# A graph network's last layer: message rows as weights, two source blocks a step, sums turned afterwards

## The reference, cut to what matters

```python
xs = x[src]; xd = x[dst]
att = sigmoid(xs @ W_att[:d] + xd @ W_att[d:] + b_att)      # one number an edge
messages = (xs @ W_msg + b_msg) * att
aggregated = segment_sum(messages, dst, num_segments=num_nodes)
# then a GRU of aggregated and x, and a batch norm
```

## Time and profile before

| | us |
|---|---|
| median of 3 runs (lowest, highest) | 6111.06 (6102.99, 6115.57) |
| the profiled execution | 6071.99 |
| its span, first to last instruction | 6069.9 |

### The profile page before, as it was taken

One profiled execution on the slowest core, in us unless ns is written; L12 is line 12 of the kernel. 1 busy time (PEld: TensorE's weight loads), 2 busy tenths in 40 slices (PEclk: granted clock), 3 DMA queues, 4 the chain that ended last, 5 costly groups with the idle time before them and its releaser, 6 DMA issues.

```text
span 6069.9 us, 111610 instructions
## 1 busy us (share of the span) xinstructions
PE 5266.9 (87%) x30743; PEld 3838.3 (63%) x30744; DVE 3972.0 (65%) x10172; ACT 2815.2 (46%) x7038; POOL 1738.2 (29%) x1720
## 2 busy tenths in 40 slices
PE   3788888999999997888888887999988998888888
PEld 2444447888888884444444445666666667777775
DVE  4999994443433335666666776555555556999996
ACT  3577772111111116777767775222222225666664
POOL 1000000000000003666666655666666660000001
PEclk8899999999999997898988887999999999999999
DMA  3355555555555532111111112333333331222220
GB/s 92 123 162 160 161 160 201 186 184 179 189 183 205 191 142 66 46 46 46 46 45 46 47 38 76 88 88 87 88 88 88 88 87 70 87 109 88 100 90 22
DMA packets 396064, 650.40 MB, mean 107 GB/s; under 512 B 99831, under 2 KB 338386, under 8 KB 370639
## 3 DMA queue, kind: packets, MB, share of 16 engines
q1 hardware_dynamic: 330844, 526.22, 25.9%
q0 software_dynamic: 54832, 117.48, 7.5%
q10 hardware_dynamic: 10052, 2.53, 0.2%
HBM read 511.57 MB, written 134.42 MB: 106 GB/s over the span
## 4 chain that ended last, share of the span: by engine, by line
PE 66%; DVE 13%; issue 9%; ACT 4%; SPq 3%; DMA 2%; DVEq 1%; another core or an unknown queue 1%; POOL 1%; ACTq 0%; POOLq 0%
PE ps L1523 20%; PE ps L1579 12%; PE ps L1714 6%; PE ps L1633 5%; PE ps L1642 4%; DVE scaled L1109 4%; PE ps L1649 3%; DVE rg L836 3%; PE ps L1635 3%; SPq L478 3%; PE ps L1636 2%; PE ps L1578 2%; PE ps L1507 2%; PE ps L1421 2%; DMA A_d<-scaled 1%
## 5 line engine op out<-in xcount | busy, mean ns | idle before, releaser
L551 POOL DMA_INDIRECT rg<-tab_L,idxT x1664 | 1649.8, 991 | 3137.5 <-DMA tab_L<-planes 2257.6
L1523 PE MATMUL ps<-planes 128*128 128x384 bf16 (+1 forms) x7350 | 1225.7, 327 | 20.1 <-DVE planes L849 16.7
L1523 PEld LDWEIGHTS ps<-planes 128*128 128x128 f16 (+1 forms) x7350 | 1036.8, 142 | 173.1 <-issue 23.5
L1265 ACT ACTIVATE scaled<-onehot,rg 128x128 f32<-128x128 f32 x2912 | 892.8, 388 | 372.9 <-PE ps L1579 190.1
L1579 PE MATMUL ps<-scaled,rg 128*128 128x512 f32 x1664 | 1018.0, 704 | 0.0
L1714 PE MATMUL ps<-planes,scaled 128*128 128x128 f32 (+1 forms) x4900 | 757.5, 298 | 89.5 <-DVE scaled L1109 89.3
L1578 PEld LDWEIGHTS ps<-rg,onehot 128*128 128x128 f32 x1664 | 335.4, 212 | 731.9 <-issue 385.3
L1109 DVE TENSOR_TENSOR scaled<-scaled,planes 128x256 f32<-128x256 f32 x1225 | 777.0, 720 | 10.6 <-DMA planes<-A_d 7.4
L1714 PEld LDWEIGHTS ps<-planes,scaled 128*128 128x128 f32 (+1 forms) x4900 | 628.7, 190 | 209.8 <-DVE scaled L1109 104.5
L1347 ACT ACTIVATE scaled<-ps,att 128x256 f32<-128x256 f32 x1225 | 568.7, 474 | 257.2 <-DVE scaled L1109 213.8
L1208 ACT ACTIVATE scaled<-ps 128x392 f16 x1184 | 549.7, 500 | 266.9 <-DMA A_d<-scaled 117.6
(11 more groups left out here) (257 smaller groups left out, 6334.4 us busy)
## 6 DMA issues: line engine op xcount, KB each, us to landing
planes<-A_d SPq DMA_DIRECT2D x196, 1568.0 KB, 8.2
A_d<-scaled SPq DMA_DIRECT2D x1184, 98.0 KB, 1.7
planes<-rows_d SPq DMA_DIRECT2D x209, 256.0 KB
rg<-tab_L,idxT POOLq DMA_INDIRECT x1664
real_row<-real_d SPq DMA_DIRECT2D x200, 32.0 KB, 4.1
planes<-w_d SPq DMA_DIRECT2D x209, 9.0 KB
tab_L<-planes SPq DMA_DIRECT2D x7, 476.0 KB, 3.1
x_keep<-planes SPq DMA_DIRECT2D x7, 448.0 KB, 3.1
```

What stands on the lines that cost most here:

```text
L551: pool.indirect_dma_start(ring[:, q * GROUP + g, 0:width], None, table[:, :], bass.IndirectOffsetOnAxis(idxT[:, at:at + 1], 0)).then_inc(g ...
L1265: last = act.activation(scaled[:, s % 4, m * P:(m + 1) * P], onehot[:, q % 2, g, :], ACT.Copy, scale=ring[:, s, D + m:D + m + 1])
L1523: last = pe.matmul(ps_agg(u), a_blk[n % ABUF][:, 0:w, k], q_rows[l % 2][:, k].rearrange("p t n -> p (t n)"), start=(k == 0), stop=(k == BL ...
```

## The change

Source blocks are taken in 25 double steps (`TWOS`), the last with one block. In each, ACT makes two gates, written side by side: `gate` is now `(set i, destination n, block k)` with k innermost and 2 long, so that ACT writes with a step of 8 bytes. DVE multiplies both with one instruction of 512 elements; of `c_blk` it reads two neighbouring fp16 at each destination. `weight` has three buffers, in the tensors `dlT`, `dlLT` and `idxT`, which hold nothing any more by then.

PE's product is turned round. The message rows of a block are the stationary operand, and the weighted counts of 256 destinations are streamed, with a step of 8 bytes. The sums come out with features on partitions (`ps_pair`). So they are turned: ACT copies them to SBUF at step `AT_LEAVE` = 1 of the next pair (`pair_sum`, semaphore `turn_in`), PE transposes them at `AT_TURN` = 3 (`turned`), and DVE's splits at 4 and 6 wait for that. The other places are halved.

```diff
-AT_PREP, AT_ATT, AT_SPLIT, AT_FOLD, AT_AGG = 28, 36, (2, 6), (16, 20), (20, 24)
+TWOS = -(-BLOCKS // 2)
+IN_TWO = [min(2, BLOCKS - 2 * h) for h in range(TWOS)]
+AT_PREP, AT_ATT, AT_LEAVE, AT_TURN, AT_SPLIT, AT_FOLD, AT_AGG = 14, 18, 1, 3, (4, 6), (9, 11), (11, 13)
...
-        gate = scaled[:, 0:2, :].rearrange("p a n -> p (a n)").rearrange("p (b k n) -> p b k n", b=4, k=2)
-        weight = scaled[:, 2:4, :].rearrange("p a n -> p (a n)").rearrange("p (b k n) -> p b k n", b=4, k=2)
-        ps_rows = lambda u: ps[0:VB_COLS[u], u % 4, 0:P]
+        gate = scaled[:, :, :].rearrange("p b (i n k) -> p b i n k", i=2, k=2)
+        weight = [t.rearrange("p (i n k) -> p i n k", i=2, k=2) for t in (dlT[:, 0:4 * P], dlLT[:, 0:4 * P], idxT[:, 0:4 * P].bitcast(fp32))]
+        ps_pair = lambda q: ps[:, q % 2, 0:2 * P]
+        pair_sum = [t[:, 4 * P:6 * P] for t in (dlT, dlLT)]
+        ps_rows = lambda u: ps[0:VB_COLS[u], 2 + u % 2, u // 2 % 2 * P:(u // 2 % 2 + 1) * P]
...
@@ DVE, split @@
-                dve.wait_ge(pair_done, BLOCKS * (u // 2 + 1))
+                dve.wait_ge(turned, u // 2 + 1)
...
@@ DVE, the loop @@
-                        if t >= 4:
-                            dve.wait_ge(pair_done, t - 3)
-                        dve.tensor_tensor(weight[:, t % 4], gate[:, t % 4], c_blk[:, 2 * q % ABUF:2 * q % ABUF + 2, :, k], ALU.mult).then_inc(weighted, 1)
+                        if t >= 3:
+                            dve.wait_ge(pair_done, t - 2)
+                        n = IN_TWO[k]
+                        dve.tensor_tensor(weight[t % 3][:, :, :, 0:n], gate[:, t % 4, :, :, 0:n], c_blk[:, 2 * q % ABUF:2 * q % ABUF + 2, :, 2 * k:2 * k + n],
+                                          ALU.mult).then_inc(weighted, 1)
...
@@ ACT, the loop @@
-                        act.activation(gate[:, t % 4].rearrange("p k n -> p (k n)"), ps_adv(q), ACT.Sigmoid, bias=att[:, k, 0:1]).then_inc(gate_ready, 1)
+                        for j in range(IN_TWO[k]):
+                            last = act.activation(gate[:, t % 4, :, :, j], ps_adv(q).rearrange("p (i n) -> p i n", i=2), ACT.Sigmoid,
+                                                  bias=att[:, 2 * k + j, 0:1])
+                        last.then_inc(gate_ready, 1)
+                    if q and k == AT_LEAVE:
+                        act.wait_ge(pair_done, TWOS * q)
+                        if q >= 3:
+                            act.wait_ge(turned, q - 2)
+                        act.activation(pair_sum[(q - 1) % 2], ps_pair(q - 1), ACT.Copy).then_inc(turn_in, 1)
...
@@ PE, the loop @@
-                            pe.wait_ge(split_done, 2 * (q - 1))
+                            pe.wait_ge(turn_in, q - 1)
                         pe.wait_ge(weighted, t + 1)
-                        for i, u in enumerate((2 * q, 2 * q + 1)):
-                            last = pe.matmul(ps_rows(u), weight[:, t % 4, i, 0:VB_COLS[u]], rows_view(3)[:, k, :], start=(k == 0), stop=(k == BLOCKS - 1))
+                        for j in range(IN_TWO[k]):
+                            last = pe.matmul(ps_pair(q), rows_view(3)[:, 2 * k + j, :], weight[t % 3][:, :, :, j].rearrange("p i n -> p (i n)"),
+                                             start=(k == 0 and j == 0), stop=(2 * k + j == BLOCKS - 1))
                         last.then_inc(pair_done, 1)
+                    if q and k == AT_TURN:
+                        pe.wait_ge(turn_in, q)
+                        if q >= 3:
+                            pe.wait_ge(split_done, 2 * (q - 2))
+                        for i, u in enumerate((2 * q - 2, 2 * q - 1)):
+                            last = pe.transpose(ps_rows(u), pair_sum[(q - 1) % 2][:, i * P:i * P + VB_COLS[u]], ident)
+                        last.then_inc(turned, 1)
```

More of the change, by code:

```diff
@@ L77 @@
 PAIRS = VB // 2
-STEPS = PAIRS * BLOCKS
-AT_PREP, AT_ATT, AT_SPLIT, AT_FOLD, AT_AGG = 28, 36, (2, 6), (16, 20), (20, 24)
+TWOS = -(-BLOCKS // 2)
+IN_TWO = [min(2, BLOCKS - 2 * h) for h in range(TWOS)]
+AT_PREP, AT_ATT, AT_LEAVE, AT_TURN, AT_SPLIT, AT_FOLD, AT_AGG = 14, 18, 1, 3, (4, 6), (9, 11), (11, 13)
 EPS = 1e-5
@@ L239, in gnn @@
         gate_ready, weighted, pair_done = sem("gate_ready"), sem("weighted"), sem("pair_done")
+        turn_in, turned = sem("turn_in"), sem("turned")
         split_step, split_done, folded, agg_out = sem("split_step"), sem("split_done"), sem("folded"), sem("agg_out")
@@ L524, in _ @@
                     if q >= 2:
-                        sp.wait_ge(weighted, BLOCKS * (q - 1))
+                        sp.wait_ge(weighted, TWOS * (q - 1))
                     sp.dma_start(c_blk[:, u % ABUF, 0:VB_COLS[u]].rearrange("p (g r) k -> p g (r k)", r=STRIP), A_d[:, u * SPB:u * SPB + k, :]).then_inc(c_in[u % ABUF], 16)
@@ L1098, in _ @@
             for q in range(PAIRS + 1):
-                for k in range(BLOCKS if q < PAIRS else AT_SPLIT[1] + 1):
+                for k in range(TWOS if q < PAIRS else AT_SPLIT[1] + 1):
                     if q < PAIRS:
-                        t = q * BLOCKS + k
+                        t = q * TWOS + k
                         if k == 0:
@@ L1338, in _ @@
             for q in range(PAIRS + 1):
-                for k in range(BLOCKS if q < PAIRS else AT_AGG[1] + 1):
+                for k in range(TWOS if q < PAIRS else AT_AGG[1] + 1):
                     if q < PAIRS:
-                        t = q * BLOCKS + k
+                        t = q * TWOS + k
                         if k == 0:
@@ L1685, in att_of @@
                 if q >= 2:
-                    pe.wait_ge(gate_ready, BLOCKS * (q - 1))
+                    pe.wait_ge(gate_ready, TWOS * (q - 1))
                 for k, u in enumerate((2 * q, 2 * q + 1)):
@@ L1706, in _ @@
             for q in range(PAIRS + 1):
-                for k in range(BLOCKS if q < PAIRS else AT_FOLD[1] + 1):
+                for k in range(TWOS if q < PAIRS else AT_FOLD[1] + 1):
                     if q < PAIRS:
-                        t = q * BLOCKS + k
+                        t = q * TWOS + k
                         if k == 0 and q >= 2:
-                            pe.wait_ge(split_done, 2 * (q - 1))
+                            pe.wait_ge(turn_in, q - 1)
                         pe.wait_ge(weighted, t + 1)
-                        for i, u in enumerate((2 * q, 2 * q + 1)):
-                            last = pe.matmul(ps_rows(u), weight[:, t % 4, i, 0:VB_COLS[u]], rows_view(3)[:, k, :], start=(k == 0), stop=(k == BLOCKS - 1))
+                        for j in range(IN_TWO[k]):
+                            last = pe.matmul(ps_pair(q), rows_view(3)[:, 2 * k + j, :], weight[t % 3][:, :, :, j].rearrange("p i n -> p (i n)"),
+                                             start=(k == 0 and j == 0), stop=(2 * k + j == BLOCKS - 1))
                         last.then_inc(pair_done, 1)
+                    if q and k == AT_TURN:
[5 more added lines that the diff above has]
+                        last.then_inc(turned, 1)
                     if q and k in AT_FOLD:
```

## The result

| | before | changed |
|---|---|---|
| median of 4 runs, us | 6111.62 | 5953.98 |
| lowest, highest | 6102.99, 6115.57 | 5950.27, 5963.54 |
| ratio, 95% interval | | 0.9746 [0.9729, 0.9763] |
| profiled span | 6069.9 | 5948.2 |
| stage, first gate to last copy of a folded block | 874.6 | 714.7 |

The kernel is 157.6 us faster; 172 were forecast, and 5939 us against 5954. The two profiled spans differ by 121.7 only, because in the second one everything ahead of the stage happened to take 38 us longer. The stage itself, where alone the code differs, is 159.9 us shorter, and that is the number to explain.

The account below looks back on a forecast made before the run. DVE's rate was taken to bound the stage at 34.6 us a pair; afterwards PE's 23.4 plus 4.4 of waits give 27.8. The stage falls from 868 to 696 us, the kernel from 6111 to 5939, range 5905 to 6020.

Parts of the forecast that it names:

- What bounds: Last layer's edge stage: DVE's own rate sets it, 34.6 us a pair of destination sets, while PE only looks full.
- DVE product, 0.72 us: DVE's product of 512 elements in a double step: 0.72 us, between bounds of 0.53 and 1.25, some pairs lying badly.
- ACT: ACT's gates and copy: 0.365 us a gate if strided writes cost nothing, copy 0.37, 18.8 us a pair.
- PE product: PE's turned product: 0.218 us a pass of 256 columns, 0.436 a block, no cost for the step, 21.4 a pair.
- Rival 1: Single words 8 bytes apart pay on PE's stream or ACT's write: slower, up to 6454 us; chance 0.13.
- my own sign: The forecast is wrong if gate or pass gets longer with its step, or pairs lie over 31 us apart.
- Transposes: PE's transposes of the turned sums: four passes of 0.111 us, 0.45 a pair.
- folds: PE's two folds a pair: six bf16 passes, 0.36 us each, 0.72 in all.
- Waits: PE waits 0.6 at the pair's start, 1.5 and 1.0 at the splits, 1.3 at folds: 4.4 us a pair.
- Sum: Whole stage: 27.8 us a pair, 868 us before to 696 after, 172 less, kernel at 5939 us.
- Rival 2: DVE pays for each element of the pair, 1.25 us a product: 34.4 a pair, 6104 us; chance 0.05.
- rival 3: PE shows half a weight load or a light charge, 0.27 us a pass: 30.7 a pair, 6012 us; chance 0.08.

Follow-up runs that it names:

- e8_turn_only: Kernel before with only PE's product turned, plus the copy and transposes this needs; single steps and DVE products of 256 stay: 5660.54 us, ratio 0.9985.
- e2_single_hops: Changed kernel with a double step's two blocks one behind the other, so DVE hops 98 bytes for every count: 5652.87 us, 0.9977 of the kernel before.
- e3_step96: Changed kernel with counts read at a step of 96 bytes in place of 98 (sums of wrong counts): 5510.78 us in one run.
- e5_places: Changed kernel with copy, transposes, splits, folds and aggregates later in the pair, preparation and attention product earlier: 5420.83 us, 0.9568 of the kernel before.
- e7_split_only: Changed kernel with copy at 6, transposes at 8, splits at 12 and 15, folds and aggregates following; preparation and attention product stay: 5857.33 us, 0.9646 of before.

## Why the prediction was right

The time lay in the range, 15 us above the forecast, and the mechanism was the one that was forecast: DVE's rate was the bound, the paired product took it away, and new waits kept PE from its own rate. By its steps:

- **What bounds.** DVE's rate was the bound; e8_turn_only and e2_single_hops change the rest, leave that rate as it was or nearly so (2.30 ns an element for 2.45), and stay within 17 us of the kernel before.
- **DVE product, 0.72 us.** Measured 0.720. The value was right, the reason wrong (e3_step96). I had picked between bounds of 0.53 and 1.25 by the nearest one plus something, and the something was put down to pairs that lie badly, which are worth 0.013 us and not 0.09. That the value came out to the third digit is luck.
- **ACT.** A gate was put at 0.365 with or without the step; it is 0.357 to 0.360 both ways. Its duration, put at 0.474, is 0.520. The copy is 0.28 of rate for 0.37.
- **PE product.** Here is the miss: a pass of 256 was put at 0.218 on the line through 128 and 448 columns, "I take no cost" for the step. Contiguous it is 0.216, with the step 0.2265. That is 98 x 0.0085 = +0.8 us a pair, 21 us in all. Rival 1 named the mechanism and priced it at up to twice the pass; it is 5%. By my own sign (a pass that got longer with its step) this part of the forecast was wrong.
- **Transposes** take one pass each, not two: 0.22 for 0.45; folds 0.33 for 0.36 each. -0.3 us a pair.
- **Waits.** Forecast 0.6, 1.5, 1.0 and 1.3, in all 4.4 us a pair. By the starts of PE's matmuls, over 20 pairs: 0.5 at steps 1 and 2, 1.6 at 4 and 5, 0.9 at 6 and 7, 1.3 to 1.5 at 10 to 15, in all 4.5. The sizes and places are right but for the last: almost nothing was waited behind the first fold. e5_places takes 3.8 of them away, e7_split_only 2.3.
- **Sum.** 22.2 + 0.9 + 0.7 + 0.2 + 4.5 = 28.5 a pair; the pairs lie 28.4 apart. Forecast 27.8. 0.6 us over the 23 pairs in the middle is 14 to 15; the first and the last pair take 25.1 and 26.4 and give 4 of it back. The stage gained 160 us for the 172 of the forecast, and the medians 158. Some 147 of the 160 lie in the 24 full pairs and 13 in the last, whose 56-column loads went (10 were forecast).
- **Rival 2** needed 1.25 for the pair, rival 3 a pass of 0.27; neither came.

By the rates for pairs in the Trainium skill (Vector Engine (DVE) Microarchitecture Reference, section 5.2) the paired product would have taken 0.54 to 0.67 us, an estimate; the trace has 0.72, and the measurement decides. The Trainium skill (Advanced Engine Details and Errata, SBUF Cachelines) has full speed where two accesses fall on one line of 16 bytes, which single words with a step of 8 bytes do. ACT's write agrees (0.357 to 0.360 us for 0.357); PE's stream and weight load do up to 5%.

## What to carry to other kernels

An element-wise instruction that reads 2-byte values a wide step apart is slow for the hops (here 2.30 ns for a hop with one value); take two neighbours that are both needed soon in one instruction, and the second is cheap (2.81 ns for a hop with two). When such a change moves the bound to another engine, list for the new bound every wait that the old one used to hide, and place each helper step where its engine still has a lead (three products, seven gates here): that was worth half as much again as the change itself, 84 us beside 164. Two bulky helpers next to each other on one engine cost 1.6 us a pair again, of the 3.8 that placing them well had saved. And look at the odd last round of a loop by itself: here a turn that cost 1.1 us or gave 0.4 in a full pair was worth 13 to 15 us in the last one.

## What the runs showed of the hardware

- DVE, 512 elements multiplied with fp16 at 98-byte hops: 1.18 us in runs of one, 0.720 in runs of two, 0.602 in runs of four; 0.707 in runs of two at 96 bytes.
- PE, fp32: a pass of 256 columns streamed takes 0.216 us contiguous and 0.2265 with a step of 8 bytes; a pass of 128 columns takes 0.112 with contiguous weights and 0.1175 with weights 8 bytes apart. Where one set of two has 56 columns, eight passes of 128 take 1.59 us for 0.94. An fp32 transpose through PE takes one pass where an fp32 product takes two.
- ACT, 256 elements written: a spacing of 0.357 us contiguous and 0.357 to 0.360 with a step of 8 bytes. The durations of such gates grow over eight in a row from 475 to 515 ns (contiguous) while the spacing stays.
- In the changed kernel PE's stalls, up to 1.5 us and 4.5 us a pair in all, left the granted clock at 1.00 (the 2.4 GHz level) from 5150 to 5845 us. In the kernel before, PE waits 11.0 us a pair, up to 1.4 at once, and the clock was 1.00 too. In e2_single_hops it waits 10.6 us a pair, up to 1.9 at once, and the clock fell to 0.50 (1.2 GHz) for some 7 us in 8 of 21 pairs, each of them 1.5 to 1.7 us longer for it.
